# Routing and dispatch in two halves, the shared FFN ahead of attention, units fetched one by one

## The reference, cut to what matters

```python
# layer 0
xn = layernorm(x)
f = xn @ W.T + b                                   # attention, b = 16 batches
a = softmax(f @ f.T + distance_bias) @ f
shared = (silu(xn @ gate.T) * (xn @ up.T)) @ down.T    # I = 256
p = sigmoid(xn @ router.T + routing_bias)          # 8 experts
scores, idx = top_k(p, 2); scores /= scores.sum()
routed = sum over the 2 chosen e: score_e * ((silu(xn @ g[e]) * (xn @ u[e])) @ d[e])
x = x + a * silu(shared + routed)
# layer 1, each 512 rows seen as in the reference
xn = layernorm(x)
s1 = attention by per-head statistics (softmax over 16 heads), then @ Wout.T
g1 = silu(xn + 0.3 * (expert FFN of the batch's one chosen expert @ Wo + bo))
x = x + s1 * g1
```

## Time and profile before

| what | value |
|---|---|
| median of 3 runs | 371.1 us |
| the profiled execution, its own time | 370.86 us |
| its span, first to last instruction | 369.0 us |
| PE / DVE / ACT / POOL busy | 301.6 / 222.2 / 183.0 / 184.1 us |
| dispatch, first to last L1230 | 43.80 to 125.8 us |
| expert stage, first turn to last L472 | 129.9 to 237.8 us |
| mean granted TensorE clock | 0.932 |

### The profile page before, as it was taken

One profiled execution on the slowest core, in us unless ns is written; L12 is line 12 of the kernel. 1 busy time (PEld: TensorE's weight loads), 2 busy tenths in 40 slices (PEclk: granted clock), 3 DMA queues, 4 the chain that ended last, 5 costly groups with the idle time before them and its releaser, 6 DMA issues.

```text
span 369.0 us, 6792 instructions
## 1 busy us (share of the span) xinstructions
PE 301.6 (82%) x1933; PEld 250.9 (68%) x1933; DVE 222.2 (60%) x722; ACT 183.0 (50%) x482; POOL 184.1 (50%) x186
## 2 busy tenths in 40 slices
PE   0896599998998089999999999997448859987880
PEld 0684386776565079999999999865125647876770
DVE  5946846655222035555655555447999775778765
ACT  2356545555532025665565565523428765565450
POOL 1220277777777506666666577716965200142432
PEclk9999969999999759999999999998959967999996
DMA  6999931111111231332323232157000032234411
GB/s 195 248 208 146 370 143 54 54 56 51 51 52 51 68 91 35 108 106 70 105 73 105 67 103 65 37 186 272 1 0 0 1 95 55 81 110 103 136 57 57
DMA packets 33187, 35.66 MB, mean 97 GB/s; under 512 B 3824, under 2 KB 26482, under 8 KB 33024
## 3 DMA queue, kind: packets, MB, share of 16 engines
q1 hardware_dynamic: 28832, 26.76, 28.1%
q0 software_dynamic: 4320, 8.47, 6.9%
HBM read 19.87 MB, written 15.80 MB: 97 GB/s over the span
## 4 chain that ended last, share of the span: by engine, by line
PE 44%; DVE 22%; POOL 15%; issue 9%; ACT 4%; DMA 3%; SPq 1%; POOLq 0%; DVEq 0%
PE PS L458 18%; POOL xs_scratch L1230 15%; PE PS L472 9%; DVE XA L657 3%; PE PS L585 3%; DVE ST L646 2%; PE PS L441 2%; PE PS L609 2%; PE PS L296 2%; DVE XG L887 2%; DVE WE L906 2%; DVE SH L827 1%; PE PS L304 1%; PE PS L288 1%; DVE F L823 1%
## 5 line engine op out<-in xcount | busy, mean ns | idle before, releaser
L1236 POOL DMA_INDIRECT yc_scratch<-YS,XS x71 | 69.8, 983 | 45.5 <-ACT YS L1098 24.7
L458 PE MATMUL PS<-XG,XB 128*128 128x128 f32 x568 | 77.3, 281 | 0.7 <-ACT XG L1086 0.7
L458 PEld LDWEIGHTS PS<-XG,XB 128*128 128x128 f32 x568 | 71.4, 198 | 1.1 <-ACT XG L1086 1.1
L800 DVE COPY XB<-WE 128x512 f32 x71 | 30.9, 435 | 34.0 <-issue 33.1
L1091 ACT ACTIVATE FT<-PS 128x256 f32<-128x256 f32 x71 | 27.3, 384 | 39.8 <-PE PS L458 39.8
L812 DVE TENSOR_TENSOR FT<-FT,PS 128x256 f32<-128x256 f32 x71 | 29.9, 421 | 24.5 <-PE PS L472 16.4
L1230 POOL DMA_INDIRECT xs_scratch<-XA,POS x32 | 31.5, 983 | 26.4 <-DVE POS L743 17.0
L472 PE MATMUL PS<-WE,FT 128*128 x284 | 43.2, 275 | 0.2 <-DVE FT L812 0.2
L472 PEld LDWEIGHTS PS<-WE,FT 128*128 128x128 f32 x284 | 37.4, 192 | 0.4 <-issue 0.4
L1230 POOL DMA_INDIRECT xs_scratch<-XB,POS x32 | 31.3, 978 | 9.8 <-issue 9.8
L1258 POOL TENSOR_TENSOR F<-F,S 128x512 f32<-128x512 f32 x7 | 8.9, 1274 | 52.6 <-DVE F L937 52.6
(11 more groups left out here) (166 smaller groups left out, 600.4 us busy)
## 6 DMA issues: line engine op xcount, KB each, us to landing
xs_scratch<-ZB SPq DMA_DIRECT2D x1, 4680.0 KB, 28.6
XS<-xs_scratch SPq DMA_DIRECT2D x17, 260.0 KB
XS<-in_w SPq DMA_DIRECT2D x16, 258.0 KB, 2.9
WE<-in_we SPq DMA_DIRECT2D x1, 3072.0 KB, 16.7
X<-in_x SPq DMA_DIRECT2D x16, 128.0 KB, 2.4
XB<-yc_scratch SPq DMA_DIRECT2D x8, 256.0 KB, 4.4
WE<-yc_scratch SPq DMA_DIRECT2D x8, 256.0 KB, 6.0
out<-X SPq DMA_DIRECT2D x16, 128.0 KB, 2.1
```

The source lines that it names most:

```text
L458: m = e.matmul(PS[k][:, f * 128:(f + 1) * 128], WC[:, u % 4, f * 128:(f + 1) * 128], XG[:, g % 2, j * 128:(j + 1) * 128], start=True, stop ...
L800: e.tensor_copy(WC[:, u % 4, :], WE[:, bass.ds(r, 512)]).then_inc(s_wc, 1)
L1236: e.indirect_dma_start(out=yc, out_offset=bass.IndirectOffsetOnAxis(ap=XS[:, g % 4, j, 128:129].bitcast(U32), axis=0), in_=YS[:, u % 8, :] ...
```

## The change

- The rows are routed in two halves, chunks 0 to 3 and chunks 4 to 7 (`CA` is 4), with the same steps on half as many numbers (`choose(g)`, `positions(g)`), and dispatched half by half. That is possible because every expert has a region of its own in `xs_scratch`, large enough for every row (`STRIDE`), so destinations need no totals. SP writes 128 rows that lead nowhere at the end of each region once the counts are known, in place of the one large fill, and `experts()` works out where each unit begins (`EI[:, 1, :]`).
- Units are fetched one by one, from an address that SP loads from `EI`.
- The shared FFN of all 8 chunks stands in front of attention, woven into the routing. `down_late`, `end0_late` and the late `up` are gone; DVE's `end0` does all 8 chunks.
- 28 matmuls on a constant tile (`warm`) stand first on PE.
- In attention the reciprocal stands behind the next batch's scores on DVE (`inverse`). The projection of chunks 4 to 7 stands in the first rounds of attention.
- ACT copies `XA` to `XB` for the second half, POOL for the first. The buffers of the stages are laid over one another anew (`EP`); `yc_scratch` of batches 8 to 15 lands in `FT`.

```diff
+CA = 4
+NTS = (4 * CA, NT - 4 * CA)
+STRIDE = NT * 128 + 128
+WARM = 28
...
-            def fetch(g):
-                n = nu[g]
-                if g >= 4:
-                    last = 4 * (g - 4) + 3
+            def fetch(u):
+                g, j = divmod(u, 4)
+                if u >= 16:
                     e.wait_ge(p_xg, g - 3)
-                    e.wait_ge(d_y[last % 8], 16 * (last // 8 + 1))
-                e.dma_start(XS[:, g % 4, 0:n, :],
-                            xs[g * 512:g * 512 + n * 128, :].rearrange("(u p) r -> p u r", p=128)).then_inc(d_xs[g % 4], 16)
+                    e.wait_ge(d_y[u % 8], 16 * ((u - 16) // 8 + 1))
+                first = e.value_load(EI[0:1, 1, u:u + 1], min_val=0, max_val=ROWS - 128)
+                e.dma_start(XS[:, g % 4, j, :], xs[bass.ds(first, 128), :]).then_inc(d_xs[g % 4], 16)
+            e.wait_ge(s_ends, 1)
+            for i in range(NE):
+                end = e.value_load(CI[0:1, i:i + 1], min_val=0, max_val=ROWS - 128)
+                e.dma_start(xs[bass.ds(end, 128), :], ZB[:, :]).then_inc(d_fill, 16)
...
+            def warm():
+                e.wait_ge(s_const, 3)
+                for _ in range(WARM):
+                    e.matmul(PS[6][:, 0:256], BFC[:, 1, 0:128], BFC[:, 1, :], start=True, stop=True)
...
+            def up(j):                                     # PE
+                c, f = divmod(j, 2)
+                k = 3 + 2 * (j % 2)
+                e.wait_ge(s_xt, c + 1)
+                if j == 0:
+                    e.wait_ge(d_wb, 16)
+                elif j >= 2:
+                    e.wait_ge(s_hh, j - 1)
...
-            for c in range(LATE, NC):
-                end0_late(c)
...
+            choose(0)                                      # DVE
+            up(0)
+            up(1)
+            positions(0)
+            for c in range(CA, NC):
+                norm0(c)
+                up(c - CA + 2)
+            choose(1)
+            up(6)
+            up(7)
+            positions(1)
+            up(8)
+            experts()
+            for j in range(9, 16):
+                up(j)
...
+            def inverse(b):
                 e.wait_ge(s_ex, b + 1)
                 e.reciprocal(SU[:, 2 * b:2 * b + 2], SU[:, 2 * b:2 * b + 2]).then_inc(s_su, 1)
...
-            for j in range(2 * LATE, 16):
-                up(j)
-                if j >= 13:
-                    end0(j - 13)
-            end0(3)
-            end0(4)
+            for c in range(NC):
+                end0(c)
...
+            def dispatch(g):                               # POOL
+                e.wait_ge(s_cols, g + 1)
+                e.wait_ge(s_places, g + 1)
...
+            dispatch(0)
+            dispatch(1)
```

More of the change, by code:

```diff
@@ L23 @@
 EPS = 1e-5
+CA = 4
+NTS = (4 * CA, NT - 4 * CA)
+STRIDE = NT * 128 + 128
+SPARE = NU - NT * 2
+ROWS = NE * STRIDE + SPARE * 128
+WARM = 28
 CW, _c = {}, 0
[L27 removed]
+for _n, _w in [("ident", 128), ("upper", 128), ("e8", 256), ("unit", 72), ("head", 16), ("lb", 8), ("dist", 512)]:
     CW[_n] = (_c, _c + _w)
@@ new lines, in down @@
+            def down(c):
+                e.wait_ge(s_hh, 2 * c + 2)
+                if c == 0:
+                    e.wait_ge(s_ft, 4)
+                else:
+                    e.wait_ge(s_sh, c)
+                for t in range(4):
+                    for f in range(2):
+                        m = e.matmul(PS[1][:, t * 128:(t + 1) * 128], HHS[:, (2 * c + f) % 3, t * 128:(t + 1) * 128],
+                                     WB[:, 512 + f * 128:512 + (f + 1) * 128], start=f == 0, stop=f == 1)
+                m.then_inc(p_dn, 1)
@@ new lines, in _ @@
+            warm()
+            turn_in(0)
+            logits(0)
+            turn_in(1)
+            logits(1)
+            project(0)
+            turn_in(2)
+            logits(2)
+            project(1)
+            turn_in(3)
+            logits(3)
+            turn_f(0)
+            up(0)
+            project(2)
+            turn_f(1)
+            up(1)
+            project(3)
+            turn_f(2)
+            turn_f(3)
+            ranks(0)
+            up(2)
+            turn_in(4)
+            logits(4)
@@ L337, in scores @@
+            up(3)
+            down(0)
+            turn_in(5)
+            logits(5)
+            up(4)
+            turn_in(6)
+            logits(6)
+            up(5)
+            down(1)
+            turn_in(7)
+            logits(7)
+            up(6)
+            up(7)
+            down(2)
+            ranks(1)
+            for j in range(8, 16):
+                up(j)
+                if j % 2 == 0:
+                    down(j // 2 - 1)
+            down(7)
             def scores(b):
@@ L426, in _ @@
-            for j in range(2 * LATE):
-                up(j)
-                if j % 2 == 0 and j > 0:
-                    down(j // 2 - 1)
-            down(LATE - 1)
             reg = {}
             def turn_x(g):
-                e.wait_ge(d_xs[g % 4], 16 * (g // 4 + 1))
+                e.wait_ge(d_xs[g % 4], 64 * (g // 4) + 16 * nu[g])
                 if g == 0:
@@ new lines, in down @@
+            def down(c):
+                e.wait_ge(p_dn, c + 1)
+                e.activation(SH[:, 4 * c:4 * c + 4, :], PS[1][:, :].rearrange("p (t d) -> p t d", d=128),
+                             ACT.Copy, bias=0.0, scale=1.0).then_inc(s_sh, 1)
+            root0(0)
+            root0(1)
+            root0(2)
+            turn_in(0)
+            root0(3)
+            turn_in(1)
+            turn_in(2)
+            project(0)
+            turn_in(3)
+            project(1)
+            root0(4)
@@ new lines, in _ @@
+            root0(5)
+            turn_f(0)
+            root0(6)
+            root0(7)
+            prob(0)
+            up(0)
+            project(2)
+            up(1)
+            turn_f(1)
+            project(3)
+            turn_f(2)
+            turn_f(3)
+            up(2)
+            turn_in(4)
+            copy_b(4)
+            up(3)
+            down(0)
+            turn_in(5)
+            copy_b(5)
+            up(4)
+            turn_in(6)
+            copy_b(6)
+            up(5)
@@ L1037, in scores @@
+            down(1)
+            turn_in(7)
+            copy_b(7)
+            prob(1)
+            up(6)
+            up(7)
+            down(2)
+            for j in range(8, 16):
+                up(j)
+                if j % 2 == 0:
+                    down(j // 2 - 1)
+            down(7)
             def scores(b):
```

647 lines of the change are left out of this document (292 added, 355 removed).

## The result

The changed kernel takes 383.36 us (median of four runs: 381.11, 382.90, 383.81, 384.29), the kernel before 371.01 on the same chip. The ratio is 1.031, with a 95% interval of 1.026 to 1.037. The forecast was 374.7, its range 366 to 380: it had the sign, and fell 8.7 us short.

A forecast was written before the change was run, and what follows sets the result against it. POOL's dispatch bounded the opening of the expert stage before; after the change PE's path would, free at 134.0. Sum: 370.86 + 0.6 to the fourth unit + 3.2 in the tail = 374.7 us, range 366.0 to 380.0.

The forecast's parts named there:

- The 28 matmuls of `warm` fill 2 to 8 us; I take them to suffice.: At the start, PE would reach its upper clock through this warm-up, with chunk 3's logits ending at 19.7 us.
- every chunk at 3.2 us of warm work: First-half routing: turn, ACT's copy, logits and a projection per chunk at PE's upper clock, about 3.2 us with handovers.
- The fall behind `experts()`: PE stands 4.0 us before 69.8 while DVE does experts(); its clock falls, charged 2.9 us more.
- the fall at 33 that I left uncharged: PE's pause of 3.2 us at 31, ahead of chunk 4; a clock fall there would cost another 0 to 2.9.
- Attention with its shorter rounds: With the reciprocal behind the next scores, attention's rounds take 2.3 us instead of 2.82; attention ends at 131.1.
- the hidden fetches: In the expert stage, SP needs about 0.7 us per single fetch against PE's 1.45 per unit: cost 0.
- the warm entry: PE enters the expert stage at its upper clock: first turn to fourth unit 4.8 us instead of 8.3.
- +3.2: Behind the expert stage, six more additions on DVE taking turns with POOL: 3.2 us more, near the saturated end.
- my upper bound of 4.4: Tail with POOL saturated: DVE's additions end at 265 instead of 260.83, given as +4.4 us.
- my saturated end: Tail case with POOL always busy: 3.0 us per chunk from 246.5 on, ending at 265.
- Rival 2: PE at its lower clock at the start, or falling at 31 too: 379 to 381 us; chance 0.15.
- Rivals 1 and 3: 1: DVE and PE interleave better before the stage, 366.5 to 368 us, 0.25; 3: POOL stays the bound, 362 to 365, 0.10.

The follow-up runs named there:

- 2: The changed kernel with 48 instead of 28 warm-up multiplications and nothing else: 382.3 us, ratio 1.034 to the kernel before.
- 5: The changed kernel without the 28 warm-up multiplications: 381.4 us, ratio 1.027 to the kernel before.
- Experiment 3: The changed kernel with 48 warm-up multiplications and 26 filler multiplications between turns and logits of the first four chunks: 375.5 us, ratio 1.007 to the kernel before.
- experiment 6: The changed kernel with the 13 operations of experts() spread ahead of the seven last up products: 377.1 us, ratio 1.021 to the kernel before.
- experiment 7: The changed kernel with the reciprocal of the row sums back in scores(): 387.8 us, ratio 1.050 to the kernel before.
- 8: The kernel before with all eight chunks of the shared FFN ahead of the expert stage and their sums on DVE: 378.7 us, ratio 1.016 to the kernel before.
- 4: The changed kernel with 26 fillers between turns and logits of the first four chunks, its 28 warm-up multiplications kept: 376.3 us, ratio 1.014 to the kernel before.
- 9: The changed kernel with the sums of the last three chunks made by PE with identity multiplications: 374.3 us, ratio 1.004 to the kernel before.

## Why the prediction was wrong, point by point

**The step that failed: "The 28 matmuls of `warm` fill 2 to 8 us; I take them to suffice."** They didn't (2, 5). With a turn, a wait of 0.69, and narrow logits for each chunk, PE lost the clock at 9.3 to 12.3 us whatever had stood ahead, and I had priced every chunk at 3.2 us of warm work. It cost 6.9 us at the last logits of chunk 3 and 6.75 at the first dispatch (40.25 for 33.5). I had the right row in hand: 1.72 us for the first logits and 0.96 later. I even said that the row of the clock couldn't be trusted there (it was no record at all, as 5 shows, so this trace doesn't bear out the warning of the Trainium skill ("TensorE: Matmul & The Clock Gate", "Seeing it yourself") against clock events), and then argued from the stage, where PE hardly stops, to a stretch in which it waits in every chunk. The Trainium skill ("TensorE: Matmul & The Clock Gate", "What you observe"), on which I leaned beside it, has the clock rise by sustained work. That agrees with these runs (the rise at 5.9 us, inside the 28 multiplications), but the work behind the warm-up has to hold the clock, and here it didn't.

**Behind that step the places came out, in part by luck.** Experiment 3 is the kernel that I had priced:

| step | forecast | experiment 3 |
|---|---|---|
| first dispatch | 33.5 | 33.23 |
| last DMA of the dispatch | 114 to 115 | 114.37 |
| end of the last `down`, with one fall of the clock | 89.1 | 88.93 |
| first turn of the stage | 134.0 | 134.08 |
| fourth unit | 138.8 | 139.06 |
| time | 374.7 | 375.5 |

These rows of experiment 3 say how it came out:

```profile
33.50 1.12 PE L310 MATMUL PS<-C,XA 128*128 128x128 f32 x4 [2.44 <-DVE XA L669]
70.25 3.39 PE L380 MATMUL PS<-WB,EP 128*128 128x128 f32 x16 [2.08 <-DVE EP L685]
86.88 2.05 PE L380 MATMUL PS<-WB,EP 128*128 128x128 f32 x16 [0.78 <-DVE EP L685]
```

The fall behind `experts()` was foreseen, but I had charged 4.0 us for the pause and 2.9 for the fall, 6.9 in all. The pause is 2.08, the fall costs some 1.8 (the `down` behind it takes 3.39 instead of 1.95, the matmuls after it 1.37 instead of 1.02), and by experiment 6 both together are worth 3.6. Against that stands the fall at 33 that I left uncharged; it came, for 1.6 to 2.0 us, and chunk 7's logits end at 54.3 instead of 52.1. The two errors cancel in the 88.93. I had judged a fall by the length of the pause, 4.0 being longer than any that was survived. Here it fell at pauses of 2.08 and 2.44, while the kernel before kept it through 3.26 (ahead of its ranks, 37.19), so the length of one pause doesn't tell.

Attention with its shorter rounds came out (44.9 forecast, 45.34 measured; 5.8 of gain by experiment 7), and so did the hidden fetches (one takes 1.9 us from issue to landing, and the stage kept its length) and the warm entry (4.8; 4.98). The time of 375.5 is partly luck as well. In experiment 3 the tail is 4.88 us longer than before, not 3.2, and the stretch from layer 1 on 1.8 shorter, which I hadn't priced; and on its chip the kernel before took 373.1 us.

**The second size: "+3.2" for the tail.** The mechanism was right, DVE and POOL by turns, but it is 5.8 to DVE's first sum into `X` (8 proves it without any of the rest), above even my upper bound of 4.4. In the trace four of the eight chunks take 3.33 to 3.35 us each (258.70 to 262.05 is one), where I had 3.0, and from the first addition at 252.55 to the sum into `X` it is 20.9 us, where my saturated end had 18.5 (246.5 to 265). The count was off: I had one and a half operations of POOL for seven chunks less the three still open, 7.5, while POOL has made nine of its twelve when the sum into `X` starts. One and a half at 1.25 are 1.9 of the 2.4 us. And I had the additions at 0.6 instead of 0.69. At the first turn of layer 1, 0.9 us of the 5.8 has been given back (+4.89).

**What I had not priced:** 1.74 us less between the first turn of layer 1 and the end. By the records of both traces PE's clock is low for 6.8 us there (309.7 to 316.5), and was for 10.2 before (298.2 to 308.4). The other kernels lie anywhere between 84.4 and 86.3 us in this stretch, with little regard to their edits (3 and 4 have 84.7 and 86.3). What goes with it is the clock: the nine traces in which it is low for 6.8 or 6.9 us have 84.4 to 84.9, the seven with 10.2 or 10.3 have 85.0 to 86.5. Which of the two an execution gets is open, as in the prologue; no run was aimed at it.

**The rivals.** Rival 2 (PE cold at the start) is what happened in mechanism. I gave it 0.15 and 379 to 381 us: too little of both, since I took +4 to +6 from it and didn't add the tail's error. Rivals 1 and 3 needed a PE faster than the lists; neither came.

## What to carry to other kernels

Price a prologue in which PE works in short bursts at the lower clock, unless a row of the same pattern shows otherwise; a warm-up in front didn't change that here, dependency-free multiplications into an unused bank in the waits did. Before work is moved from the tail of a stage, look at which engine takes over what it did beside it: the three chunks on PE cost at most 2.4 us where they were (9), and DVE paid 5.8 us for the sums that came with their move. Where DVE and POOL both add or multiply SBUF tiles of 128x512, add their times.

## What was not expected of the hardware

- PEclk says 1.00 ahead of the first record of the clock, also while PE is at half pace: without any warm-up the logits took 1.87 us at 10.87 and 14.38, and the first record is the rise at 19.0. Up to there the durations decide.
- Without a difference in the instructions the clock came back at about 19 us in some executions and at 29 to 31.5 in others, 3 to 5 us at the first dispatch.
- A tensor_tensor of 128x512 on DVE beside one on POOL: 0.69 and 1.26 us alone, 1.56 to 1.78 both together; bn_stats (4 in 0.84 alone) took 0.87 there.
- On one chip all kernels took 21 to 23% longer, by stops that no instruction or DMA of the profile explains.
